# First attention of a macaron block: whole weighted sums between two row pairs, row steps listed by width

## The reference, cut to what matters

```python
q, k, v = (proj(Wq), proj(Wk), proj(Wv))        # 16 heads of 16 columns, 1024 tokens, 2 sequences
q = _apply_rope(q, cos, sin); k = _apply_rope(k, cos, sin)
scores = jnp.einsum('bhqd,bhkd->bhqk', q, k) / math.sqrt(hd)
scores = scores + causal                        # -inf above the diagonal
probs = jax.nn.softmax(scores, axis=-1)
ctx = jnp.einsum('bhqk,bhkd->bhqd', probs, v)
x = x + ctx @ Wo.T
```

## Time and profile before

| | us |
|---|---|
| three runs: median (lowest to highest) | 2808.95 (2788.56 to 2831.16) |
| the profiled execution: device time, span | 2803.01, 2801.2 |
| PE busy in the span | 2578.4 (92%) |
| DVE, ACT busy | 1845.3 (66%), 1409.6 (50%) |
| mean granted clock of TensorE | 0.946 of full speed |

### The profile page before, as it was taken

One profiled execution on the slowest core, in us unless ns is written; L12 is line 12 of the kernel. 1 busy time (PEld: TensorE's weight loads), 2 busy tenths in 40 slices (PEclk: granted clock), 3 DMA queues, 4 the chain that ended last, 5 costly groups with the idle time before them and its releaser, 6 DMA issues. The chain is left out here.

```text
span 2801.2 us, 51262 instructions
## 1 busy us (share of the span) xinstructions
PE 2578.4 (92%) x17384; PEld 2142.4 (76%) x17384; DVE 1845.3 (66%) x4006; ACT 1409.6 (50%) x2466; POOL 360.7 (13%) x277
## 2 busy tenths in 40 slices
PE   3985999969899999996899999999999599999999
PEld 3863455448788888886778878878778588888888
DVE  4566667545576777765677767767667666776773
ACT  3421445645455555553455555555555455555553
POOL 1000000010022222212101001001100212222220
PEclk9985679869999999998999999999999799999999
DMA  4025133000000000000000000000000000000000
GB/s 153 0 84 135 24 47 48 2 31 1 31 30 1 31 30 30 0 1 19 20 20 1 19 11 8 19 0 19 19 0 31 31 1 31 31 30 0 30 0 30
DMA packets 18930, 73.30 MB, mean 26 GB/s; under 512 B 3328, under 2 KB 8192, under 8 KB 15616
## 3 DMA queue, kind: packets, MB, share of 16 engines
q1 hardware_dynamic: 18816, 71.78, 8.9%
HBM read 61.02 MB, written 10.49 MB: 26 GB/s over the span
## 5 line engine op out<-in xcount | busy, mean ns | idle before, releaser
L316 PEld LDWEIGHTS ps<-w,hid 128*128 128x128 f32 x5376 | 698.7, 191 | 54.2 <-DVE rb L388 15.4
L316 PE MATMUL ps<-w,hid 128*128 128x256 f32 x5376 | 719.3, 284 | 0.9 <-DVE hid L462 0.9
L291 PE MATMUL ps<-xT,w 128*128 (+1 forms) x2688 | 704.8, 398 | 0.0
L462 DVE TENSOR_TENSOR hid<-gel,hid 128x512 fp32r<-128x512 f32 x448 | 395.0, 892 | 366.9 <-ACT hid L357 358.2
L351 ACT ACTIVATE gel<-ps,b 128x512 f32<-128x512 f32 x448 | 306.9, 686 | 559.5 <-issue 546.6
L291 PEld LDWEIGHTS ps<-xT,w 128*128 128x128 f32 x2688 | 480.2, 190 | 79.0
L357 ACT ACTIVATE hid<-gel 128x512 fp32r<-128x512 f32 x448 | 272.9, 622 | 0.0
L745 PE MATMUL ps<-pT,v_sb 128*128 128x512 f32 (+3 forms) x1152 | 260.1, 356 | 1.3 <-DVE pT L848 1.3
L718 PE MATMUL ps<-k_sb,q_sb 128*128 128x512 f32 (+3 forms) x1152 | 251.5, 351 | 1.5 <-DVE q_sb L865 1.4
L1287 DVE TENSOR_REDUCE nmx<-ps 128x1 f32<-128x512 f32 (+3 forms) x384 | 196.0, 552 | 78.3 <-PE ps L1154 47.2
L837 DVE TENSOR_REDUCE negmax<-ps 128x1 f32<-128x128 f32 (+7 forms) x256 | 192.5, 752 | 78.7 <-PE ps L721 77.5
(11 more groups left out here) (111 smaller groups left out, 2999.9 us busy)
## 6 DMA issues: line engine op xcount, KB each, us to landing
wraw<-in_wffn SPq DMA_DIRECT2D x11, 2048.0 KB, 7.7
xb<-in_w_a SPq DMA_DIRECT2D x8, 1280.0 KB, 5.5
qk_dram<-rope_hl SPq DMA_DIRECT2D x16, 512.0 KB, 3.0
xT<-qk_dram SPq DMA_DIRECT2D x60, 128.0 KB, 8.3
xb<-in_wffn SPq DMA_DIRECT2D x3, 2048.0 KB, 9.4
qk_own<-qk_dram SPq DMA_DIRECT2D x36, 128.0 KB, 6.7
x<-in_x SPq DMA_DIRECT2D x4, 512.0 KB, 5.6
rot<-in_rot SPq DMA_DIRECT2D x1, 2048.0 KB, 18.7
```

The costliest lines, as they stand in the source:

```text
L291: last = nc.tensor.matmul(ps[:, HPS + j % 4, :], w[par][:, wp, 0, k * HIDDEN + j * PART:k * HIDDEN + (j + 1) * PART], xT[:, xp, k, bass.ds ...
L316: last = nc.tensor.matmul(y_ps[:, t, :], hid[:, hp, j % 4, t * PART:(t + 1) * PART], w[par][:, wp, 1, j * DIM:(j + 1) * DIM], start=j == 0 ...
L462: nc.vector.tensor_tensor(hid[:, 1, j % 4, :], gel[:, j % 4, :], hid[:, 0, j % 4, :].bitcast(f32), ALU.subtract).then_inc(low_done, 1)
```

## The change: what it does

The loop of `plan_a0` now makes one turn for each step instead of each pair. A step issues both turned pairs, the first row pair, the weighted sum of the step behind it in one piece, and the second row pair. `weighted` loses its halves: each of its four matmuls is now as wide as the step. `AV_LAG` is now 1 step (it was 4 pairs). The words C, E and O are put down in steps. `ROW_STEPS` is a list written out: 512, 384, 256, 128 (all with a causal part), the same once more, and then the four plain steps. Since the row pairs are still eight pairs ahead, a wide turned step now has wide row pairs beside it and a narrow one narrow ones, and the plain turned steps have the plain row steps.

```diff
-        ROW_STEPS = [(qt, kc) for qt in range(QT) for kc in range(qt // 4 + 1)]
+        ROW_STEPS = [(3, 0), (2, 0), (1, 0), (0, 0), (7, 1), (6, 1), (5, 1), (4, 1), (4, 0), (5, 0), (6, 0), (7, 0)]
         T_GROUP = 2 * len(TILE_STEPS)
-        AHEAD, AV_LAG = 8, 4
+        AHEAD, AV_LAG = 8, 1
...
-            for i in range(last_t + AV_LAG + 4):
-                if i < last_t:
-                    todo.append(("T", i // T_GROUP, i % T_GROUP // 2, i % 2))
-                j = i + T_GROUP + AHEAD
+            def rows_beside(i, half):
+                j = T_GROUP + AHEAD + 2 * i + half
                 if j < last_t:
                     rows_of(j)
                 elif j == last_t + 1:
                     todo.append(("N", GROUPS - 1))
-                if 0 <= i - AV_LAG < last_t:
-                    step, half = divmod(i - AV_LAG, 2)
-                    g, s = divmod(step, len(TILE_STEPS))
-                    todo.append(("A", g, s, half))
+
+            for i in range(steps + AV_LAG):
+                if i < steps:
+                    todo += [("T", i // len(TILE_STEPS), i % len(TILE_STEPS), p) for p in range(2)]
+                rows_beside(i, 0)
+                if i >= AV_LAG:
+                    g, s = divmod(i - AV_LAG, len(TILE_STEPS))
+                    todo.append(("A", g, s))
                     qc, kt = TILE_STEPS[s]
-                    if half and kt == 4 * qc + 3:
+                    if kt == 4 * qc + 3:
                         todo.append(("X", g, qc))
-                        late.setdefault(i + 2, []).append(("C", g, qc))
+                        late.setdefault(i + 1, []).append(("C", g, qc))
                         if qc and g % GROUP == GROUP - 1:
                             b = g // GROUP
                             for n in range(4):
-                                late.setdefault(i + 3 + n, []).append(("E", b, n // 2, n % 2))
-                                late.setdefault(i + 8 + n, []).append(("O", b, n))
+                                late.setdefault(i + 2 + n // 2, []).append(("E", b, n // 2, n % 2))
+                                late.setdefault(i + 4 + n // 2, []).append(("O", b, n))
+                rows_beside(i, 1)
                 todo += late.pop(i, [])
...
-            def weighted(g, s, half):
+            def weighted(g, s):
                 qc, kt, q0, width, _ = tile_step(s)
                 step = len(TILE_STEPS) * g + s
-                if width == PART and not half:
-                    return
-                cols = slice(0, width) if width == PART else slice(half * width // 2, (half + 1) * width // 2)
                 pe.wait_ge(t_exp, 2 * step + 2)
...
-                if half:
-                    last.then_inc(av0_done, 1)
+                last.then_inc(av0_done, 1)
```

More of the change, by code:

```diff
@@ L1091, in plan_a0 @@
                 rows_of(j)
-            late = {}
-            for i in range(last_t + AV_LAG + 4):
-                if i < last_t:
-                    todo.append(("T", i // T_GROUP, i % T_GROUP // 2, i % 2))
-                j = i + T_GROUP + AHEAD
+            late, steps = {}, last_t // 2
+            def rows_beside(i, half):
+                j = T_GROUP + AHEAD + 2 * i + half
                 if j < last_t:
@@ L1202, in weighted @@
                     at = (g % GROUP * GROUP + h) * VW
-                    last = nc.tensor.matmul(ps[mine, AV0_PS, q0 + cols.start:q0 + cols.stop],
+                    last = nc.tensor.matmul(ps[mine, AV0_PS, q0:q0 + width],
                                             v_f[:, g // GROUP * QT + kt, at:at + 32],
-                                            pT0[:, step % P_STEPS, h, cols], start=kt == 0 and not half,
-                                            stop=kt == 4 * qc + 3 and half == 1, skip_group_check=True)
-                if half:
-                    last.then_inc(av0_done, 1)
+                                            pT0[:, step % P_STEPS, h, 0:width], start=kt == 0,
+                                            stop=kt == 4 * qc + 3, skip_group_check=True)
+                last.then_inc(av0_done, 1)
             def turn_maxima(g):
```

## The result

The change takes **2778.5 us**, median of 20 runs (2771.96 to 2800.65); the kernel before takes 2810.4 in 20 runs (2775.8 to 2849.05). The ratio of the runs is 0.9934, with a 95% interval of 0.9908 to 0.996: faster, by less than 2% but clear of its uncertainty. The forecast was 2811, that is, no change. (The ratio leaves out the runs of before that were over 1.5% above its fastest, which is why it shows less than the medians.)

What follows compares the result with a forecast made beforehand. The prediction took PE to set the time. Terms at an unchanged clock, -21 + 7 + 13 + 1.6, were put at 0; with +8 for the clock, 2803 + 0 + 8 = 2811 us, range 2772 to 2850.

Steps and rivals of the forecast that it cites:

- part 4: PE's clock: five falls after pauses, each about 24 us until the plain steps, 44 us lost against 37 before: +8.
- The sum at an unchanged clock: All terms except the clock's, over the whole kernel: -21 + 7 + 13 + 1.6 = 0.
- Part 1, fewer turns and fixed parts: PE's weighted sums and shape turns: 2.6 us a group saved at full clock, 21 us in eight groups.
- Part 2, waits for DVE: Wide row maxima beside wide turned steps: PE waits 1.0 us more a group (bounds 0 and 2.4), 7 us in all.
- Part 3, pauses of 2.0 us: PE waits for the maxima's DMAs at each of seven group changes, 2.0 us each: about +13 us against before.
- The chain from the turned maxima: Turned maxima through DVE and SP's DMAs to the turned pair needing them: 8.2 us before, forecast 8.5.
- the stretch: PE's work from the turned maxima to the next group's first turned pair: 8.63 us before, forecast 6.5.
- The first group: Wider row maxima ahead of its turned maxima make the turned pairs start 1.6 us later.
- five of seven pauses: At the group changes, five of seven pauses of 2.0 us were to bring PE's clock down.
- The first rival: Every pause at the seven group changes brings the clock down: +25, 2828 us; chance 0.22.
- The second rival: The clock holds in all groups after the first: -37, 2766 us; chance 0.15.
- the signs to look for: Profile after: 2 us pauses, five or more short low stretches, 512-column sum 0.99 us, groups 32 to 33 us, about 41 with a fall.

Runs made afterwards that it cites:

- a_again: The change itself run once more, nothing altered: median 2780.3 us, ratio to before 0.9969.
- a_halves: The change with each wide weighted sum issued as two halves directly behind each other: 2785.8 us, ratio to before 0.9965.
- a_old_rows_again: Second set of runs of the change with the old list of row steps: 2775.6 us, ratio to before 0.9948.
- b_new_rows: The kernel before with only the new list of row steps: 2843.5 us, ratio to before 1.0121.
- b_ahead6: The kernel before with row pairs six ahead instead of eight: 2869.0 us, ratio to before 1.0243.
- a_apart: The change with each weighted sum cut into halves again, one on each side of the second row pair: 2819.2 us, ratio to before 1.0118.
- a_apart_old_rows: The change with the sum's halves on either side of the second row pair and the old row list: 2824.9 us, ratio to before 1.011.
- b_halfmax: The kernel before with DVE reading half the columns of each row for its maximum: 2761.9 us, ratio to before 0.9888.
- a_halfmax: The change with DVE reading half the columns of each row for its maximum: 2771.5 us, ratio to before 0.9927.
- a_ahead10: The change with row pairs ten ahead instead of eight: 2777.3 us, ratio to before 0.9925.
- a_ahead6: The change with row pairs six ahead instead of eight: 2802.4 us, ratio to before 1.0007.

## Why the prediction was wrong

The time fell into the range (2772 to 2850), but the forecast of no change did not hold. **The step that failed is part 4**: a fall of the clock was to last "about 24 us". In the profile it lasted 6.8 us, four times: 27 us where I had five times 24 and before had 100. One execution of a_again has 23.9 us once and 3.4, 6.8 and 6.8 for the others, and those of a_halves and a_old_rows_again have stretches of 20.5 and 23.9 too, so 24 us does occur and was no rule. Over the runs the low clock is 60 us less than before (242 against 302); at 0.35 that is 21 us, and the medians beside each other in the table differ by 21.5. My reasoning was from the plain steps without causal parts, and it failed as such: the clock rose at 391.6 ahead of them, and at 507.7 it fell in the midst of them. What the runs show instead is that a step's weighted sum in one place makes the difference: with full maxima, low clock was 302 to 476 us where the halves are apart (before, b_new_rows, b_ahead6, a_apart, a_apart_old_rows), and 227 to 286 where the sum is in one place (eleven sets of runs, the one in halves and the one with pauses of 2.6 us among them). It is no law: b_halfmax has its halves apart and only 237 us of low clock, a_halfmax has whole sums and 277. Where DVE holds PE up less, the clock depends on something else, and why it answers to the place of the sum at all is not shown.

**The sum at an unchanged clock was 0, and it measured -1** (2778.5 against 2779.5). That it fits so well is luck: the saving was put 9 us too high and the pauses 9 too high as well. Its terms can be read with the half maxima, where DVE's waits are nearly gone:

- *Part 1, fewer turns and fixed parts, -21.* The difference of the two kernels with half maxima is -5.5, and in it the change pauses 8.4 us for the DMAs and before 2.0. So what is left, PE's work first of all, shrank by about 12 us, 1.5 a group. The single prices held (0.99 forecast for a sum of 512, 1.00 measured; 0.57 for 256, 0.57). That merging alone (a_halves against after) gave 2.4 us and not 11 hints at where they went: they are prices of a PE that waits for nobody.
- *Part 2, waits for DVE, +7.* The full maxima cost the change 19.2 us and before 14.7; with the pauses that come and go (8.4 against 6.5, and 2.0 against 2.8) that is 21.1 against 13.9: +7.2. The size was right. The place was not only the wide steps: PE waits for DVE already in the stretch with narrow pairs (310.25). The list of waits, by itself, says +16. The Trainium skill, TensorEngine Tiling (Array Packing), PSUM Bottleneck, warned of this; the trace agrees in kind, but the 2.4 us a group that would be paid in full by it were too much for what was new.
- *Part 3, pauses of 2.0 us, +13.* They were 0.40, 0.42, 0.98, 0.41, 0.70, 0.43 and 2.92: 6.3 us, +3.5 against before. The chain from the turned maxima was 316.89 - 308.71 = 8.2 us and not 8.5, and the stretch held 7.8 us of PE and not 6.5; 0.8 of that were waits for DVE (0.43 at 310.25 and two of under 0.2), which I had not put into this part. Here the waits for DVE filled part of the pause for the DMAs.
- *The first group, +1.6.* The turned pairs start no later (275.52 against 275.82), but the group takes 41.4 us instead of 39.6: +1.7, for another reason than mine (0.4 of it is the pause). It is contained in the terms above.

-12 + 7 + 4 is -1. It has to be, since the terms are differences of the same four times; what they show is how the -1 comes about, each to some 3 us.

**The clock's falls.** I had five of seven pauses bring it down, being 2.0 us each. Three did, of 0.70, 0.98 and 2.92 us, and once it fell with no such pause. The pause of 1.00 of before, which left the clock up, thus set no edge; nor is a pause for the maxima needed (a_ahead10). The first rival, that every pause brings it down, holds in a_ahead6, where all are over 2.6; the Trainium skill, TensorE: Matmul & The Clock Gate, HAM oscillation, has that rule for waits of 3 to 5 us, and there the trace agrees, from 2.6 us on. It doesn't tell that one order pays 7 to 10 us of low clock for it and another 24 to 82, and this is what decided here. The second rival, the clock that holds (2766, 0.15), was the nearest in time and half right in its reason.

**Of the signs to look for**, a group at full clock of 32 to 33 us came (32.7), with short falls instead of long ones, and the price of a sum. The pauses of 2 us did not, and a group with a fall takes about 35 us, not 41 (382.87 to 417.95 is 35.1).

## What to carry to other kernels

Where TensorE's clock moves in the trace, split the runs by their mean granted clock before explaining a difference: here two orders that take the same time at the same clock differ by 21 us in the median, and in the profiles the cause lay in how soon the clock came back, not in how often it fell. A saving on PE's instructions is worth its price only as far as the engine that empties PSUM keeps up; make that engine cheaper once in an experiment to see what it really holds back, since the list of waits told 3 us where 15 were to be had. And try each part of a change alone: the list of rows by width, one of its two ideas, is a small loss in the new order and costs 40 us in the old one.

## What the runs showed of the hardware

- PE stayed at 1.2 GHz while busy for 124.6 of 126.3 us (b_new_rows) and 60.7 of 61.4 (before), and came back from 1.2 GHz after 6.8 us elsewhere (after). Being busy was not what told these apart (PE was busy for 6.50 of those 6.80 us); where the halves of a weighted sum stand was.
- Two halves of a weighted sum right behind each other leave 253 us of low clock, the same halves with one row pair between them 330, on another chip; with the old rows it is 344 against 244 for the whole sum on the same chip. The reason stays open, as do the falls without a pause for maxima, at 507.7 us and three in a_ahead10.
- A microsecond at 1.2 GHz costs this kernel 0.35 us over many runs, near the 0.37 from two groups of one profile. It explains nearly all of its spread of 73 us.
- The DMAs of a group's maxima, eight small ones, take 5.39 us on SP's queue (5.9 at the most), and where PE waits for them it is 7.5 to 8.8 us from the turned maxima to the pair that needs them, in either order (9.7 once, before 479.52).
